# Linear attention with a running state: inter and state product in 64x32 tiles over pairs of sequences, and a new order of the steps around them

## The chip, the cores and the metric

The kernel runs on one core of a Trainium2 chip. The metric is the device time of one execution in microseconds (us), the median of the runs. A core has a matrix engine (TensorE, here PE), whose results go to PSUM banks, and VectorE (DVE), ScalarE (ACT) and GpSimd (POOL); SyncE (SP) issues DMAs. Every engine works through its own list of instructions in order and waits on semaphores.

## What is computed

Input: x of 4 sequences by 2048 tokens by 512 features. It is normalised (xn), and the result is x + attention(xn) + fp8 layer(xn):

```python
q = softmax(be * heads(xn @ Wq.T + bq));  k = softmax(be * heads(xn @ Wk.T + bk));  v = heads(xn @ Wv.T + bv)
kv = cumsum(einsum('zsD,zsd->zsDd', k, v), axis=1);  kn = cumsum(k, axis=1)      # 64 heads of 8
out = einsum('zsD,zsDd->zsd', q, kv) / sum(q * kn)
attention = out @ Wo.T + bo
ffn = fp8(clip(xn / input_scale)) @ (weight_fp8 * weight_scale).T + bias
```

## The kernel before

A step takes 32 tokens (TOK) of each of the 4 sequences (SEQS), so 128 rows; there are 64 steps. The sum over the past is split: *intra* is the product of a step's masked scores with its own values, *inter* the product of the queries with the running state (k times v and, as a ninth column, k times one, hence VW = 9, summed over all steps before). The 64 heads are held as 16 groups g of J = 4 heads: a 32x32 block transposition on DVE (`qT`, `kT`) puts 4 heads times 8 features on 32 partitions, one band of 32 partitions for each sequence.

Every engine runs `body(i)` for i = 0 to 65, each with three ages of step in flight: i (projections), t = i - 1 (scores, state, inter, intra) and i - 2 (output). PE's order in `body(i)` (L921) is: keys of i into `k_ps`, scores half 0 of t, `state(t, 0)`, transposition of the attention of i - 2 (L943), queries of i into `q_ps`, scores half 1, `state(t, 1)`, fp8 product (L975) and output product (`project_out`, L884 to L888) of i - 2 into `vo_ps`, inter of t (L999), values of i into `vo_ps` (L873 to L877 with another target), intra of t (L1018). A projection is 12 float16 matmuls of 512 columns (`project`).

- `state` (L905 to L919): for each group and sequence a 32x32 product of `k_e` and `vp` over the rows of that sequence, 36 columns; the four sequences lie on the diagonal of the array. The result holds, for each sequence's band, 4 heads against 4 heads, of which DVE keeps the diagonal (`mask_state`, L650) and adds it to `st_run` (`add_state`, L660).
- The spread (ACT, L530): `st_run` is copied four times, each time with one sequence's band kept (`seq_mask`), into `st_seqs`, so that a row of it has a block of 36 columns for each sequence.
- inter (L999): 128 rows (all sequences) by 32 columns of `qT`, with 144 columns of `st_seqs`. It writes into `a_ps`, which the state product used before it, and waits for `masked_ready`.
- intra (L1018): 64 matmuls, 128x32, of 36 columns, added to the same bank.
- The output's bias is put into `vo_ps` by ACT (L477, after the values were read), the keys' bias into `k_ps` (L489, right after the exponential of the keys).
- DVE's order in `body(i)` (L731 on): attention of i - 2 divided by its sum (L682, L690), `xn` of i + 1, quantising of i (L637), maximum and shift of k, two score masks, first state mask, `al` (low part of the attention, L748), key sums and `kT`, shift of q, `magic` (L624, L629), two score masks, `qT` (L769), second state mask, output (L720), `add_state`, statistics of i + 3, variances (each second step), values times 1/sum (`vp`, L727).
- POOL makes the low part of the input (L400), the rounding of the fp8 input (L407, L411) and the root (L385 to L391). SP issues the DMAs in a fixed order: 8 for the values of t, two transposing ones, input, output, residual.

## Time and profile before

| | |
|---|---|
| median of 3 runs | 1249.07 us (1248.55 to 1250.06) |
| profiled execution | 1248.2 us from its first to its last instruction, 60447 instructions |
| PE busy | 1174.9 us (94%) |
| DVE busy | 977.9 us (78%) |
| ACT busy | 744.9 us (60%) |
| POOL busy | 321.6 us (26%) |

The profile is one execution. Its page lists the busy time of each engine, the chain of work that ended last, and groups of instructions by line; the trace behind it can be asked for a stretch of time, an engine or a line. A matmul's record shows its latency, several hundred ns; the time that a series of them takes is read from the starts. A float32 matmul has two records, a float32 transposition one, a float16 matmul one.

### The profile page before, as it was taken

What the parts mean: (1) busy time and instruction counts of PE and PEld (TensorE: products, weight loads), DVE (VectorE), ACT (ScalarE), POOL (GpSimd) and SP (SyncE); (2) the same over time, 40 slices, a digit from 0 to 9 for tenths busy, and PEclk for the clock granted to TensorE, in tenths of its full rate; (3) what the DMA queues carried; (4) which work ended last, traced back from release to release, by engine and by line L of the source; (5) the groups of instructions that cost most, each with busy time, mean ns of one, the idle gap of its engine ahead of it and who ended that gap; (6) DMA issues with size and microseconds to landing.
All of it is one profiled execution on the core that took longest, in us unless ns stands there. A gap on an engine that the chain in (4) does not pass through costs nothing.

```text
span 1248.2 us, 60447 instructions
## 1 busy us (share of the span) xinstructions
PE 1174.9 (94%) x26082; PEld 679.2 (54%) x26082; DVE 977.9 (78%) x1968; ACT 744.9 (60%) x1177; POOL 321.6 (26%) x590
## 2 busy tenths in 40 slices
PE   1459999999999999999999999999999999999996
PEld 1235555555555555555555555555555555555553
DVE  4567887888788788878878887788788778878873
ACT  0456656665666666566666656666665666566652
POOL 3122222322222232222223232222323232222310
PEclk9689999999999999999999999999999999999999
DMA  9022334334334433433333343343343433333331
GB/s 234 21 59 70 81 90 89 78 80 91 82 82 87 89 80 79 90 86 80 85 89 82 77 90 89 78 84 91 81 79 91 84 83 81 91 82 81 72 73 46
DMA packets 156483, 104.64 MB, mean 84 GB/s; under 512 B 111968, under 2 KB 128480, under 8 KB 156256
## 3 DMA queue, kind: packets, MB, share of 16 engines
q1 hardware_dynamic: 155536, 99.76, 35.7%
q8 instruction: 209, 3.42, 1.2%
q10 hardware_dynamic: 720, 1.31, 0.4%
q14 instruction: 18, 0.15, 0.0%
HBM read 40.20 MB, written 16.78 MB: 46 GB/s over the span
## 4 chain that ended last, share of the span: by engine, by line
PE 92%; issue 3%; DVE 2%; DMA 1%; ACT 1%; POOL 1%; SPq 0%; POOLq 0%; DVEq 0%; ACTq 0%
PE s_ps L900 10%; PE a_ps L917 7%; PE a_ps L1018 6%; PE a_ps L999 6%; PE k_ps L873 5%; PE vo_ps L975 5%; PE vo_ps L873 5%; PE k_ps L877 5%; PE k_ps L875 5%; PE vo_ps L884 4%; PE vo_ps L888 4%; PE vo_ps L886 4%; PE vo_ps L877 4%; PE vo_ps L875 4%; PE q_ps L877 4%; PE q_ps L873 4%
## 5 line engine op out<-in xcount | busy, mean ns | idle before, releaser
L521 ACT ACTIVATE q_heads<-qT,cst 128x512 f32<-128x512 f32 x256 | 163.9, 711 | 88.2 <-DVE qT L769 88.2
L407 POOL TENSOR_TENSOR y_sum<-y,y_magic 128x512 f32<-128x512 f32 x64 | 81.4, 1272 | 433.0 <-DVE y_magic L629 433.0
L506 ACT ACTIVATE w_own<-kT,cst 128x512 f32<-128x512 f32 x128 | 85.5, 715 | 166.7 <-DVE kT L711 166.7
L530 ACT ACTIVATE st_seqs<-st_run,cst 128x576 f32<-128x576 f32 x252 | 181.5, 797 | 0.5 <-DVE st_run L665 0.5
L671 DVE TENSOR_TENSOR att<-s_ps,cst 128x512 f32<-128x512 f32 x256 | 163.8, 682 | 0.4 <-PE s_ps L900 0.4
L400 POOL TENSOR_TENSOR x_split<-xn,x_split 128x512 f16<-128x512 f32 x64 | 74.1, 1158 | 291.6 <-ACT x_split L462 284.3
L900 PE MATMUL s_ps<-q_heads,w_own 64*64 64x128 f32 x4096 | 141.3, 275 | 0.6 <-DVE att L671 0.6
L900 PEld LDWEIGHTS s_ps<-q_heads,w_own 64*64 64x64 f32 x4096 | 110.4, 132 | 54.3 <-issue 54.2
L462 ACT ACTIVATE x_split<-xn 128x512 f16<-128x512 f32 x64 | 40.3, 630 | 126.7 <-DVE xn L618 126.7
L873 PE MATMUL k_ps<-w_hi,xT 128*128 128x512 f16 x256 | 98.9, 386 | 17.0 <-DMA xT<-x_split 12.3
L727 DVE TENSOR_TENSOR vp<-vo_ps,vp 128x512 f32<-128x512 f32 x64 | 44.3, 692 | 86.3 <-PE vo_ps L877 86.3
L884 PE MATMUL vo_ps<-w_hi,ah 128*128 128x512 f16 x260 | 98.5, 379 | 0.6 <-DVE al L748 0.6
L888 PE MATMUL vo_ps<-w_hi,al 128*128 128x512 f16 x260 | 98.5, 379 | 0.0
L886 PE MATMUL vo_ps<-w_lo,ah 128*128 128x512 f16 x260 | 98.5, 379 | 0.0
L875 PE MATMUL k_ps<-w_lo,xT 128*128 128x512 f16 x256 | 98.3, 384 | 0.0
L877 PE MATMUL k_ps<-w_hi,xT 128*128 128x512 f16 x256 | 98.3, 384 | 0.0
L873 PE MATMUL vo_ps<-w_hi,xT 128*128 128x512 f16 x256 | 97.7, 382 | 0.0
L917 PE MATMUL a_ps<-vp,k_e 32*32 32x36 f32 x8064 | 97.6, 196 | 0.0
L873 PE MATMUL q_ps<-w_hi,xT 128*128 128x512 f16 x256 | 97.0, 379 | 0.0
L875 PE MATMUL q_ps<-w_lo,xT 128*128 128x512 f16 x256 | 97.0, 379 | 0.0
L877 PE MATMUL q_ps<-w_hi,xT 128*128 128x512 f16 x256 | 97.0, 379 | 0.0
L875 PE MATMUL vo_ps<-w_lo,xT 128*128 128x512 f16 x256 | 97.0, 379 | 0.0
(136 smaller groups left out, 2287.8 us busy)
## 6 DMA issues: line engine op xcount, KB each, us to landing
v_groups<-vp SPq DMA_DIRECT2D x512, 36.0 KB, 3.1
x_in<-L_attn_x SPq DMA_DIRECT2D x64, 256.0 KB
x_res<-L_attn_x SPq DMA_DIRECT2D x64, 256.0 KB
out<-o_sb SPq DMA_DIRECT2D x64, 256.0 KB
w_own<-L_attn_Wk SPq DMA_DIRECT2D x1, 1024.0 KB, 13.0
w_own<-L_attn_Wq SPq DMA_DIRECT2D x1, 1024.0 KB, 15.0
w_own<-L_attn_Wv SPq DMA_DIRECT2D x1, 1024.0 KB, 16.5
att<-L_ffn_weight_fp SPq DMA_DIRECT2D x1, 1024.0 KB, 18.1
```

Of the source, the lines that this page charges most:

```text
L506: last = sc.activation(k_pairs[:, i.parity, :, c, :], kT[:, :, :], ACT.Copy, scale=pair_mask[:, c:c + 1])
L521: last = sc.activation(q_heads[:, i.parity, :, j, :], qT[:, i.parity, :, :], ACT.Copy, scale=head_mask[:, j:j + 1])
L530: last = sc.activation(st_seqs[:, i.parity, :, :, b, :].rearrange("p g j w -> p (g j) w"), st_run[:, :, :, :].rearrange("p g j w -> p (g j ...
L671: v.tensor_tensor(att[:, c % 2, 4 * (c // 2):4 * (c // 2) + 4, :, :] .rearrange("p g j s -> p (g j) s"), s_ps[:, DM * (c % 2):DM * (c % 2 ...
L873: mm(bank[:, :], xT[:, t.parity, 0, c, :], w_hi[:, m, c, :], start=(c == 0 and not seeded), stop=False, skip_group_check=seeded)
L875: mm(bank[:, :], xT[:, t.parity, 0, c, :], w_lo[:, m, c, :], start=False, stop=False, skip_group_check=seeded)
L877: last = mm(bank[:, :], xT[:, t.parity, 1, c, :], w_hi[:, m, c, :], start=False, stop=(c == KC - 1), skip_group_check=seeded)
L884: mm(vo_ps[:, :], ah[:, j, :], w_hi[:, MO, j, :], start=(j == 0 and not rest), stop=False, skip_group_check=rest)
L886: mm(vo_ps[:, :], ah[:, j, :], w_lo[:, MO, j, :], start=False, stop=False, skip_group_check=rest)
L888: last = mm(vo_ps[:, :], al[:, j, :], w_hi[:, MO, j, :], start=False, stop=(j == J - 1), skip_group_check=rest)
L900: last = mm(s_ps[SP * TOK * gp:SP * TOK * (gp + 1), DM * n + P * q:DM * n + P * (q + 1)], k_pairs[rows, t.parity, g, :, :].rearrange("p c ...
L917: last = mm(a_ps[rows, col:col + J * VW], k_e[rows, t.parity, TOK * g:TOK * (g + 1)], vp[rows, t.parity, v_head(g):v_head(g) + J, :], star ...
```

## The change

- The state product is formed for pairs of sequences: 64 rows (two sequences) by 32 columns of `k_e`, with 72 columns: a new tile `v_pairs` holds the values twice, once with only the even and once with only the odd sequences' rows (`pair_mask`), so that the two come out side by side. 32 matmuls in place of 64, in one stage after scores half 0. The new rows' band is the group within its four (u), not the sequence.
- POOL makes `v_pairs` with two multiplications (`pair_values`) ahead of its other work of a step; `state` waits for them.
- `mask_state` handles both halves at once. The spread moves blocks between bands of 32 partitions: 16 small copies in place of 4 large ones, in two halves, one at the end of a body and one in the next body, after `ah`.
- inter is 32 matmuls of 64x32 with 72 columns; bank n of `a_ps` now holds a pair of sequences. intra keeps its matmuls and is called in two halves with waits of their own.
- The fp8 and the output product go into `k_ps`; the output's seed follows the exponential of the keys, and the keys' seed waits for DVE's output. `vo_ps` holds only values, which wait for `vp` of the step before.
- DVE's order: statistics ahead of `xn`; both state masks after the first score masks; variances and `magic` ahead of `al`; output ahead of `qT`; quantising for i + 1 near the end.

The diff, cut to its core:

```diff
-        st_seqs = sb("st_seqs", [P, 2, G, J, SEQS, VW])
...
+        v_pairs = w_own[0][:, :, :].rearrange("p c d -> p (c d)")[:, 0:SP * HEADS * VW]\
+            .rearrange("p (c h w) -> p c h w", c=SP, h=HEADS)
+        st_masked = sb("st_masked", [P, SEQS // SP, G // J, SP, J, VW])
+        st_run = sb("st_run", [P, SEQS // SP, G // J, SP, J, VW])
+        st_pairs = sb("st_pairs", [P, 2, G, J, SP, VW])
...
-        a_view = a_halves[:, :, 0:G // 2 * GW]
-        a_rows = a_view.rearrange("p n (l r) -> p n l r", l=GP)
+        a_view = a_halves[:, :, 0:G * SP * VW]
+        a_rows = a_view.rearrange("p n (h l j r) -> p n h l j r", h=2, l=GP, j=J)
...
+            def pair_values(t):
+                pool.wait_ge(vp_ready, (t + 1).n)
+                if t.after(1):
+                    pool.wait_ge(state_done, t.n)
+                for c in range(SP):
+                    last = gp.tensor_tensor(v_pairs[:, c].rearrange("p h w -> p (h w)"),
+                                            vp[:, t.parity].rearrange("p h w -> p (h w)"),
+                                            pair_mask[:, c:c + 1].to_broadcast([P, HEADS * VW]), ALU.mult)
+                last.then_inc(vpairs_ready, 1)
             def body(i):
...
                     low_input(i + 1)
...
@@ -465,28 +482,41 @@
...
+            def spread_state(t, seqs):
...
+                if seqs[0] == 0:
+                    act.wait_ge(strun_ready, (t + 1).n)
+                    if t.after(1):
+                        act.wait_ge(a_done, t.n)
+                    else:
+                        act.wait_ge(st_cleared, 1)
+                for b in seqs:
+                    for u in range(J):
+                        last = sc.activation(st_pairs[TOK * b:TOK * (b + 1), to, u::J, :, b % SP, :],
+                                             st_run[TOK * u:TOK * (u + 1), b // SP, :, b % SP, :, :],
+                                             ACT.Copy)
+                if seqs[-1] == SEQS - 1:
+                    last.then_inc(stpairs_ready, 1)
...
             def body(i, last_weights=None, fold=False):
-                t = i - 2
-                if t.exists():
-                    if (t + 1).exists():
-                        act.wait_ge(vp_ready, (t + 2).n)
-                    else:
-                        act.wait_ge(o_ready, t.n)
-                    if t.off == 0 and isinstance(t.k, int):
-                        act.wait_ge(fold_ready, 1)
-                    sc.activation(vo_ps[:, :], bias[:, 3, :], ACT.Copy, scale=out_up[:, :])\
-                        .then_inc(oseed_ready, 1)
+                d = i - 2
                 if (i + 1).exists():
                     high_input(i + 1)
                 if i.exists():
                     act.wait_ge(kshift_ready, (i + 1).n)
                     if i.after(2):
-                        act.wait_ge(state_done, (i - 1).n * 2)
+                        act.wait_ge(state_done, (i - 1).n)
                         act.wait_ge(kT_ready, (i - 1).n)
                     sc.activation(k_e[:, i.parity, :], k_shift[:, :], ACT.Exp, scale=k_exp_scale[:, :])\
                         .then_inc(ke_ready, 1)
-                    if (i + 1).exists():
-                        sc.activation(k_ps[:, :], bias[:, MK, :], ACT.Copy).then_inc(kseed_ready, 1)
+                if d.exists():
+                    if not i.exists():
+                        act.wait_ge(o_ready, d.n)
+                    if d.off == 0 and isinstance(d.k, int):
+                        act.wait_ge(fold_ready, 1)
+                    sc.activation(k_ps[:, :], bias[:, 3, :], ACT.Copy, scale=out_up[:, :])\
+                        .then_inc(oseed_ready, 1)
...
+                if d.exists() and (i - 1).exists():
+                    spread_state(d, range(SP, SEQS))
...
                     if (i + 1).exists():
                         sc.activation(q_ps[:, :], bias[:, MQ, :], ACT.Copy).then_inc(qseed_ready, 1)
+                        if d.exists():
+                            act.wait_ge(o_ready, (d + 1).n)
+                        sc.activation(k_ps[:, :], bias[:, MK, :], ACT.Copy).then_inc(kseed_ready, 1)
...
                     last.then_inc(qheads_ready, 1)
...
-                    for b in range(SEQS):
-                        last = sc.activation(st_seqs[:, i.parity, :, :, b, :].rearrange("p g j w -> p (g j) w"),
-                                             st_run[:, :, :, :].rearrange("p g j w -> p (g j) w"),
-                                             ACT.Copy, scale=seq_mask[:, b:b + 1])
-                    last.then_inc(stseqs_ready, 1)
+                if (i - 1).exists() and i.exists():
+                    spread_state(i - 1, range(SP))
...
-            def mask_state(t, n):
-
...
+            def mask_state(t):
+                dve.wait_ge(state_done, (t + 1).n)
+                for n in range(SEQS // SP):
+                    last = v.tensor_tensor(
+                        st_masked[:, n].rearrange("p q c j w -> p (q c) j w"),
+                        a_state[:, n, :].rearrange("p (g j w) -> p g j w", j=J, w=VW),
+                        head_mask[:, None, :, None].to_broadcast([P, G // 2, J, VW]), ALU.mult)
...
             def body(i, last_weights=None, fold=False):
-                t = i - 1
-                if (i - 2).exists():
-                    normalise_attention(i - 2)
+                t, d = i - 1, i - 2
+                if d.exists():
+                    normalise_attention(d)
+                if (i + 3).exists():
+                    statistics(i + 3)
                 if (i + 1).exists():
                     normalise(i + 1)
                 if i.exists():
-                    if i.after(1):
-                        quantise(i)
                     shift(i, k_ps, k_done, k_max, kmax_ready, k_shift, kshift_ready, ke_ready)
                 if t.exists():
                     mask_scores(t, 0)
                     mask_scores(t, 1)
-                    if i.exists():
-                        mask_state(t, 0)
-                if (i - 2).exists():
-                    dve.wait_ge(ah_ready, (i - 1).n)
-                    v.tensor_tensor(flat(al[:, :, :]), t_ps[:, :], flat(ah[:, :, :]), ALU.subtract)\
-                        .then_inc(al_ready, 1)
+                if t.exists() and i.exists():
+                    mask_state(t)
+                if i.parity == 0 and (i + PAIR).exists():
+                    variances(i + PAIR)
+                if (i + 1).exists():
+                    magic(i + 1)
+                if d.exists():
+                    split_low(d)
...
                 if i.exists():
                     key_sums(i)
+                if i.exists():
                     shift(i, q_ps, q_done, q_max, qmax_ready, q_shift, qshift_ready, qe_ready)
-                if (i + 1).exists():
-                    magic(i + 1)
                 if t.exists():
                     mask_scores(t, 2)
                     mask_scores(t, 3)
-                if i.exists():
-                    dve.wait_ge(qe_ready, (i + 1).n)
-                    if i.after(2):
-                        dve.wait_ge(qheads_ready, (i - 1).n)
-                        dve.wait_ge(a_done, (i - 1).n)
-                    v.transpose(qT[:, i.parity].rearrange("p g s -> p (g s)"), q_e[:, :]).then_inc(qT_ready, 1)
-                if t.exists() and i.exists():
-                    mask_state(t, 1)
...
-                if (i - 2).exists():
-                    output(i - 2)
+                if d.exists():
+                    output(d)
+                if i.exists():
+                    turn_queries(i)
                 if t.exists() and i.exists():
                     add_state(t)
-                if (i + 3).exists():
-                    statistics(i + 3)
-                if i.parity == 0 and (i + PAIR).exists():
-                    variances(i + PAIR)
+                if (i + 1).exists():
+                    quantise(i + 1)
                 if i.exists():
                     scale_values(i)
...
-            def state(t, n):
-
...
+            def state(t):
...
+                pe.wait_ge(ke_ready, (t + 1).n)
+                pe.wait_ge(vpairs_ready, (t + 1).n)
...
+                pe.sem_inc(pe_waited, 1)
+                for c4 in range(G // J):
+                    for u in range(J):
+                        g = J * c4 + u
+                        for n in range(SEQS // SP):
+                            rows = slice(SP * TOK * n, SP * TOK * (n + 1))
+                            col = DM * n + SP * J * VW * c4
+                            last = mm(a_ps[TOK * u:TOK * (u + 1), col:col + SP * J * VW],
+                                      k_e[rows, t.parity, TOK * g:TOK * (g + 1)],
+                                      v_pairs[rows, :, v_head(g):v_head(g) + J, :]
+                                      .rearrange("p c j w -> p c (j w)"), start=True, stop=True)
+                last.then_inc(state_done, 1)
...
+            def values(i, fold):
...
+                if i.after(1):
+                    pe.wait_ge(vp_ready, i.n)
+                project(vo_ps, i, MV, seeded=False).then_inc(v_done, 1)
...
+            def quantised(t, low_part):
...
+                pe.wait_ge(xq_turned, (t + 1).n * 16)
+                pe.wait_ge(oseed_ready, (t + 1).n)
+                for c in range(KC):
+                    last = mm(k_ps[:, :], xq[:, t.slot, c, :], w_hi[:, MF, c, :], start=False,
+                              stop=False, skip_group_check=True)
...
+            def output_product(t):
...
+                pe.wait_ge(ah_ready, (t + 1).n)
+                pe.wait_ge(al_ready, (t + 1).n)
+                project_out(k_ps, rest=True).then_inc(o_done, 1)
...
+            def inter(t, more):
+                pe.wait_ge(qT_ready, (t + 1).n)
+                if more:
+                    pe.wait_ge(masked_ready, (t + 1).n)
...
+                if t.after(1):
+                    pe.wait_ge(stpairs_ready, t.n)
+                pe.sem_inc(pe_waited, 1)
+                for h in range(2):
+                    for gp in range(GP):
+                        for u in range(J):
+                            g = G // 2 * h + GP * u + gp
+                            for n in range(SEQS // SP):
+                                rows = slice(SP * TOK * n, SP * TOK * (n + 1))
+                                mm(a_rows[TOK * u:TOK * (u + 1), n, h, gp].rearrange("p j r -> p (j r)"),
+                                   qT[rows, t.parity, g, :],
+                                   st_pairs[rows, t.parity, g].rearrange("p j c w -> p (j c w)"),
+                                   start=(h == 0 and gp == 0), stop=False, skip_group_check=True)
+            def intra(t, h):
+                pe.wait_ge(att_ready, t.n * 4 + 2 * h + 2)
+                if h == 0:
+                    for b in range(SEQS):
+                        pe.wait_ge(v_moved[t.parity][b], (t + 2).half * 16 * GP)
                     pe.sem_inc(pe_waited, 1)
...
+                for n in range(SEQS // SP):
+                    for j in range(J):
+                        for u in range(J):
+                            last = mm(a_rows[TOK * u:TOK * (u + 1), n, h, :, j, :],
+                                      att[:, n, J * h + u, j, :],
+                                      v_groups[:, t.parity, :, n, J * h + u, j, :], start=False, stop=True,
+                                      skip_group_check=True)
+                if h == 1:
+                    last.then_inc(a_done, 1)
```

## Rows read from the trace of the kernel before

**Rows 1.** Page: busy time, chain by engine; span and mean granted clock.

```profile
PE 1174.9 (94%) x26082; PEld 679.2 (54%) x26082; DVE 977.9 (78%) x1968; ACT 744.9 (60%) x1177; POOL 321.6 (26%) x590
...
PE 92%; issue 3%; DVE 2%; DMA 1%; ACT 1%; POOL 1%; SPq 0%; POOLq 0%; DVEq 0%; ACTq 0%
...
core 0: 1248.2 us, clock 0.982
```

**Rows 2.** Stretch: busy PE, PEld, DVE, ACT, POOL; PEclk, DMA share, GB/s.

```profile
500.00:600.00 100.00, 99.36 (x2261) 57.55 (x2260) 82.39 (x168) 60.95 (x97) 26.71 (x52) 1.00 0.39 88
```

**Rows 3.** PE in order of time: intra of bodies 1, 2, 63.

```profile
98.32 1.31 PE L1018 MATMUL a_ps<-v_groups,att 128*32 128x36 f32 x128
...
117.17 1.32 PE L1018 MATMUL a_ps<-v_groups,att 128*32 128x36 f32 x128
...
1223.53 1.31 PE L1018 MATMUL a_ps<-v_groups,att 128*32 128x36 f32 x128
```

**Rows 4.** As rows 2: inter, values, intra; keys to second state.

```profile
603.24:604.36 1.12, 1.12 (x33) 0.90 (x33) 1.05 (x2) 1.12 (x3) 0.51 (x1) 1.00 0.01 4
604.36:607.06 2.70, 2.70 (x17) 1.10 (x13) 1.15 (x3) 2.70 (x5) 0.00 (x0) 1.00 0.19 18
607.06:608.34 1.28, 1.28 (x129) 1.23 (x129) 0.69 (x1) 1.28 (x3) 0.00 (x0) 1.00 0.23 51
...
608.34:611.02 2.68, 2.68 (x15) 1.07 (x13) 2.12 (x6) 1.07 (x3) 0.00 (x0) 1.00 0.37 113
611.02:612.05 1.03, 1.03 (x33) 0.86 (x32) 0.89 (x2) 0.57 (x1) 0.92 (x1) 1.00 0.37 130
612.05:612.75 0.70, 0.70 (x69) 0.65 (x65) 0.70 (x2) 0.04 (x1) 0.25 (x1) 1.00 0.45 134
612.75:613.24 0.49, 0.49 (x11) 0.48 (x6) 0.49 (x2) 0.49 (x1) 0.00 (x0) 1.00 0.32 102
613.24:615.92 2.68, 2.68 (x14) 1.08 (x12) 2.15 (x4) 1.20 (x3) 0.00 (x0) 1.00 0.54 110
615.92:616.96 1.04, 1.04 (x34) 0.87 (x33) 0.91 (x2) 0.00 (x0) 0.00 (x0) 1.00 0.79 136
616.96:617.73 0.77, 0.77 (x69) 0.72 (x65) 0.77 (x2) 0.52 (x1) 0.00 (x0) 1.00 0.76 156
```

**Rows 5.** Waits from 500 to 1100 us (us in total, times, longest).

```profile
PEld s_ps L900 <- issue: 28.0, 66, 0.4
PEld a_ps L999 <- DVE qT L769: 17.8, 31, 0.7
```

**Rows 6.** Order of time around inter; DVE's first and last of a step.

```profile
602.72 0.42 DVE L654 TENSOR_TENSOR st_masked<-a_ps,cst 128x288 f32<-128x288 f32 x1
...
608.42 0.57 DVE L682 RECIPROCAL den_rec<-a_ps 128x32 f32<-128x32 f32 x2 [0.50 <-PE a_ps L1018]
...
621.01 0.42 DVE L654 TENSOR_TENSOR st_masked<-a_ps,cst 128x288 f32<-128x288 f32 x1
...
625.45 0.69 DVE L727 TENSOR_TENSOR vp<-vo_ps,vp 128x512 f32<-128x512 f32 x1 [1.09 <-PE vo_ps L877]
...
620.98 0.38 PE L888 MATMUL vo_ps<-w_hi,al 128*128 128x512 f16 x1
621.53 1.19 PE L999 MATMUL a_ps<-st_seqs,qT 128*32 128x144 f32 x32 [0.17 <-issue]
```

**Rows 7.** ACT in order of time: one column, 512 columns, the spread of a step.

```profile
4.95 0.20 ACT L454 ACTIVATE exp_beta<-scal 128x1 f32<-128x1 f32 x1 [2.94 <-DMA scal<-L_ffn_weight_scale]
...
51.70 0.58 ACT L569 ACTIVATE q_ps<-bias 128x512 f32<-128x512 f32 x1
...
605.30 2.88 ACT L530 ACTIVATE st_seqs<-st_run,cst 128x576 f32<-128x576 f32 x4
```

**Rows 8.** Groups by line on POOL (busy us, mean ns, idle before).

```profile
L407 POOL TENSOR_TENSOR y_sum<-y,y_magic 128x512 f32<-128x512 f32 x9 | 11.5, 1273 | 62.7 <-DVE y_magic L629 62.7
...
L436 POOL TENSOR_TENSOR bias<-bias,w_scale_up 128x512 f32<-128x512 f32 x2 | 2.0, 1028 | 6.9 <-issue 6.9
```

More of the change, by code:

```diff
@@ L892, in scores @@
             def scores(t, half):
+                if half == 0:
+                    pe.wait_ge(kpairs_ready, (t + 1).n)
+                    pe.wait_ge(qheads_ready, (t + 1).n)
+                    if t.after(1):
+                        pe.wait_ge(att_ready, t.n * 4)
+                else:
+                    pe.wait_ge(att_ready, t.n * 4 + 2)
                 pe.sem_inc(pe_waited, 1)
@@ new lines, in turn_attention @@
+            def turn_attention(t):
+                pe.wait_ge(an_ready, (t + 1).n)
+                if t.after(1):
+                    pe.wait_ge(al_ready, t.n)
+                else:
+                    pe.wait_ge(bvl_ready, 1)
+                for b in range(SEQS):
+                    last = transpose(t_ps[:, :].rearrange("p (j b s) -> p b j s", b=SEQS, s=TOK)[:, b],
+                                     a_n[:, b, :, :].rearrange("p g d -> p (g d)"), ident)
+                last.then_inc(aT_done, 1)
@@ L932, in body @@
                     scores(t, 0)
                     if i.exists():
[L934 to L945 removed]
+                        state(t)
@@ L946, in body @@
+                if d.exists():
+                    turn_attention(d)
                 if fold:
@@ L1024, in transpose_weights @@
+                    inter(t, i.exists())
+                if i.exists():
+                    values(i, fold)
+                if t.exists():
+                    intra(t, 0)
+                    intra(t, 1)
             def transpose_weights(m):
```

188 lines of the change are left out of this document (63 added, 125 removed).

## The prediction

> **What bounds the kernel now.** I read the page first: one engine, the matrix engine (PE), is busy 94% of the span, at a mean granted clock of 0.982, so at the higher of its two levels (2.4 GHz), and the chain that ended last is 92% PE [rows 1]. Then the busy time of a steady stretch: in 100 us PE is busy 99.36, VectorE (DVE) 82.39, ScalarE (ACT) 60.95, GpSimd (POOL) 26.71 [rows 2]. So in the loop only PE's own work counts, and everything else matters as far as it makes PE wait. The step: intra starts at 98.32 in body 1 and 1223.53 in body 63 [rows 3], that is 1125.2 us in 62 steps, 18.15 each, and without the slow first one (117.17 to 1223.53, 61 steps) 18.14. 63 bodies have all stages; the start-up ends at about 80 us.
>
> Next the stages of one step in PE's order [rows 4]: keys 2.68, scores 1.03, state 0.70, turning of the attention 0.49, queries 2.68, scores 1.04, state 0.77, then fp8 and output products (617.73 to 621.29, with the usual 0.31 from the last matmul [rows 6]: 3.56), inter 1.12, values 2.70, intra 1.28. The float16 products are untouched, at 12 matmuls of 512 columns in 2.68. The float32 stages consist of passes (two records for each float32 matmul, one for each transposition), and here the rows give a price per column: scores 32 passes of 128 columns in 1.03 us = 0.25 ns a column; inter 32 of 144 in 1.12 = 0.24; state 64 of 36 in 0.70 to 0.77 = 0.30 to 0.33; intra 128 of 36 in 1.28 = 0.28. All four spread over four tiles of the array (64x64; 128x32; the four diagonal 32x32; 128x32). The transposes take the whole array as one tile: 4 passes of 128 columns in 0.49 = 0.96 ns a column, 3.9 times the four-tile price. For the shortest passes the floor is per pass: 10.0 ns (intra), 10.9 and 12.0 ns (state).
>
> PE's only true wait in the loop is before inter: PE's load of weights is idle 17.8 us over 31 times there, 0.57 each, while at scores the idle time is 28.0 over 66, 0.42 each [rows 5]. The 0.15 beyond the usual pause are a wait. The row names the transposition of the queries (L769), but that had ended; what ends last is the second masking of the state (L654, ends 603.14, and inter starts at 603.24; in the next step ends 621.43, inter 621.53) [rows 6]. In the second of these it costs 0.24 us: the last output matmul starts at 620.98, and a change of stage elsewhere costs 0.31. I take 0.14 a step.
>
> **The change on PE.** State before: 64 matmuls = 128 passes of 36 columns in two stages, 0.70 + 0.77 = 1.47. After: 32 matmuls = 64 passes of 72 columns, in one stage. Inter before: 16 matmuls = 32 passes of 144, 1.12. After: 32 matmuls = 64 passes of 72. Both then have the same form: 4608 pass-columns in 64x32 tiles, of which the array holds eight. No row shows this form. The nearest rows bound it. If eight tiles stand to four as four to one, a column costs 0.12 and the stage 0.56; the floor per pass, 64 x 10.0 to 12.0 ns, gives 0.64 to 0.77. If the array gives no more than the four-tile price, 4608 x 0.243 = 1.12. I take 0.70, the length of the state stage that also has 64 passes [rows 4], because from one tile to four the price fell almost in proportion. So state saves 1.47 - 0.70 = 0.77, inter 1.12 - 0.70 = 0.42.
>
> The Trainium skill says the first too: "TensorEngine Tiling (Array Packing)", Tiling Modes, lists 64x32 as eight tiles that load and multiply independently; the trace bears that out up to four. Against the change speaks "TensorE: Matmul & The Clock Gate", Part 1, on the 56 ns gap, which puts matmuls never closer than about 25 ns from start to start: 64 passes would take 1.6 us, the two stages 3.2 against 2.6 now, some 0.6 us a step slower. This trace disagrees, with 128 passes in 1.28 us, so the rule gets no chance of its own.
>
> The wait of 0.14 goes, since both maskings now follow the first masks of the scores: state is done at 4.4 us of the step (below), masked by 6.2, and inter starts at 12.2. Intra keeps its 64 matmuls of the same shape. Sum for a step: 0.77 + 0.42 + 0.14 = 1.33; 18.14 becomes 16.8.
>
> **Does the rest keep up?** I lay out a new step, keys at 0: scores 2.7, state 3.7, turn 4.4, queries 4.9, scores 7.6, fp8 8.6, output 9.5, inter 12.2, values 12.9, intra 15.6, end 16.8.
>
> DVE has the same operations of the same sizes: 82.39% of 18.14 = 14.9 us, against 16.8. In its new order, with the durations of its timeline (28 rows for one step, the first and the last in [rows 6]): normalising the attention from 0.1 to 1.35, statistics to 2.4, xn to 2.8 (keys are done at 2.8), k's shift to 4.2, masks to 5.4, both state maskings to 6.2, variances (each second step, 0.6) to 6.9, magic to 7.7, al to 8.4, key sums and kT to 10.4, q's shift to 11.7, masks to 12.9, output to 13.6, qT to 14.2, state sum to 14.8, quantising to 15.3. Then it waits for the values (15.7) and for intra. The tight places for PE: al at 8.4 against the output product at 9.5, and an idle rest of 1 us in even steps. Nothing on DVE delays PE, so the reordering itself costs and gains nothing beyond the 0.14.
>
> ACT: four spreads of 576 columns, 2.88 us [rows 7], become 16 copies of 32 partitions and 144 columns. Bounds of one: 0.20 (the 1-column row) and 0.58 (512 columns) [rows 7]; linear between them 0.31. Sixteen cost 5.0 at most where the old cost 2.9: ACT goes from 11.1 to 13.2 of 16.8. The second half (after ah, at 6.4) ends by 8.9, before kT at 10.4 and before inter at 12.2; the first half follows q_heads and ends early in the next step, before xn at 2.8. Cost nothing, hidden by 3 us.
>
> K's bank: the output's seed goes in after k_e, about 5.8, against 8.6. The seed for the next keys waits for the output (13.6) and is in by 14.2, against 16.8; q_heads behind it on ACT wait for qT at 14.2 anyway and end at 16.8, against scores 2.7 later. Values no longer wait for the output, which would have been late: output done 12.3 plus 0.75 after an inter of 0.70. So this move costs nothing and keeps 0.2 from coming back.
>
> POOL: two new multiplications of 576 columns. The nearest rows are 1.03 (512, with a broadcast factor) and 1.27 (two tensors) [rows 8], so 1.16 to 1.43 each, 2.3 to 2.9 together. They start after vp, 0.4 before keys, and end by 1.9 to 2.5; state needs them at 3.7. Behind them on POOL wait the low input (its own input comes at 3.9) and so the transposing DMA, which has until 16.8. The cover is 1.2 us or more.
>
> The granted clock is 1.00 in all these stages and PE stays busy, so I expect it unchanged. Start-up: the same; in body 1 the wait before inter (0.75) goes.
>
> **Sum.** State 63 x 0.77 = 48.5, inter 64 x 0.42 = 26.9, waits 62 x 0.14 + 0.75 = 9.4: 84.8 us. The profiled span 1248.2 becomes 1163.4; the median of the runs (1249.07) is 0.9 above that span: 1164.
>
> **Rivals.**
> (a) Four-tile price. The array has four float32 streams at a time, whatever the tiles; nothing in the trace shows more than four. For it: every float32 stage fits one price per column; against it: the one-tile row. Then state saves 1.47 - 1.12 = 0.35, inter nothing: 22.1 + 9.4 = 31.5, that is 1218.
> (b) DVE becomes the bound. POOL's 2.3 us fall on DVE's busiest stretch. If DVE lost all of it, its 14.9 and 0.3 of handshakes become 17.5, and the step with them: 0.64 x 63 = 40, that is 1209. The Trainium skill's "GPSIMD Engine Reference", Key points, says that the two share their SBUF interfaces; the trace has POOL idle during most of this stretch and can't show it.
> (c) Slower: the two row bands of a column band write the same PSUM partitions, in two banks, and take turns. Each of the two stages then runs at half the four-tile price, 2.24: 4.48 against 2.59 + 0.14, or 1.75 a step, 110 us: 1359. It decides from 21 ns a pass on. Scores, with two row bands on the same partitions in two banks, cost 0.25 a column, which speaks against it.
> (d) The change doesn't do what it says: a new wait (state for POOL's pairs: their cover of 4.1 us plus 1.33 is used up at 2.7 us an operation) eats all of the gain. No change, about 1249.
>
> **Chances.** Forecast 0.57, (a) 0.27, (b) 0.10, (c) 0.03, (d) 0.03. Low end: both stages at 0.60, 12 us less, 1152. High end takes in (a) with some us for small waits: 1223. A measurement of this kernel can tell about 0.2% from no change. Faster 0.94, same 0.02, slower 0.04.
>
> **What would show it.** Stage windows of state and inter near 0.70 each (right), 1.1 (a), 2.2 (c). Intra to intra 16.8. PE still over 99% busy in the loop, DVE near 89%. If DVE is near 98% and PE has gaps before the output product or the keys, (b). If PE is idle before state behind POOL's new line, (d). Copies of 144 columns above 0.5 us, or POOL's above 2 us, would make my covers wrong.

## The result and the profile after

The changed kernel takes 1187.03 us (median of 4 runs, 1185.41 to 1187.85), the kernel before 1249.57 in the same session. The ratio is 0.9492, with a 95% interval of 0.9477 to 0.9507: 62.5 us faster, where 84.8 were forecast (1164). The forecast case was the right one, and the size is three quarters of it. The profiled span is 1185.7 us.

The page of the kernel after (busy time of PE and the others, the chain by engine, span and granted clock) answers to [rows 1]:

```profile
PE 1115.6 (94%) x24098; PEld 627.9 (53%) x24098; DVE 967.9 (82%) x1968; ACT 899.3 (76%) x1933; POOL 463.6 (39%) x717
...
PE 91%; issue 4%; DVE 2%; DMA 2%; POOL 1%; SPq 0%; ACT 0%; POOLq 0%; DVEq 0%
...
core 0: 1185.7 us, clock 0.982
```

The steady stretch, columns as in [rows 2]:

```profile
500.00:600.00 100.00, 100.00 (x2205) 55.94 (x2188) 85.42 (x177) 81.62 (x178) 42.19 (x66) 1.00 0.47 88
```

PE has no gap left in this stretch, so it still bounds the kernel. DVE is at 85%, ACT went from 61 to 82%, POOL from 27 to 42%. Intra in bodies 1 and 63, for [rows 3]:

```profile
98.64 1.31 PE L1045 MATMUL a_ps<-v_groups,att 128*32 128x36 f32 x128
...
1160.73 1.31 PE L1045 MATMUL a_ps<-v_groups,att 128*32 128x36 f32 x128
```

That is 1062.1 us in 62 steps, 17.13 each, against 18.15: the gain of a step is 1.02 where 1.33 were forecast, and 1.02 x 62 = 63 is the whole gain. The start-up and the end got longer by 0.3 us each. The stages of one step, in the order scores, state, turning, queries, then inter, values, intra (for [rows 4]):

```profile
601.14:602.18 1.04, 1.04 (x34) 0.87 (x33) 1.00 (x3) 0.63 (x2) 0.00 (x0) 1.00 0.42 133
602.18:602.99 0.81, 0.81 (x68) 0.71 (x64) 0.81 (x2) 0.81 (x3) 0.65 (x1) 1.00 0.39 132
602.99:603.48 0.49, 0.49 (x10) 0.48 (x5) 0.49 (x2) 0.49 (x2) 0.49 (x1) 1.00 0.46 139
603.48:606.17 2.69, 2.69 (x15) 1.08 (x12) 2.66 (x7) 2.62 (x8) 0.58 (x2) 1.00 0.63 142
...
610.76:611.58 0.82, 0.82 (x65) 0.71 (x65) 0.71 (x2) 0.00 (x0) 0.00 (x0) 1.00 0.19 70
611.58:614.27 2.69, 2.69 (x18) 1.08 (x12) 1.64 (x4) 2.60 (x5) 0.00 (x0) 1.00 0.18 18
614.27:615.53 1.26, 1.26 (x130) 1.21 (x129) 0.69 (x1) 1.24 (x4) 0.29 (x1) 1.00 0.16 36
```

State and inter take 0.81 and 0.82 each; all other stages are what they were. The clock is 1.00 in all of them. The waits from 500 to 1100 us (us in total, times, longest), for [rows 5]:

```profile
DVE vp L754 <- PE vo_ps L911: 35.4, 35, 1.2
ACT k_ps L550 <- DVE o_sb L747: 33.3, 35, 1.3
...
PEld s_ps L941 <- issue: 29.7, 70, 0.4
...
PEld a_ps L1030 <- issue: 14.8, 35, 0.4
```

Before inter (L1030) the load of weights now pauses 14.8 over 35 times, 0.42 each, as long as before scores (29.7 over 70). The wait before inter is gone. DVE's idle time ahead of `vp` (1.0 us a step) comes back in the experiment with the statistics and variances late. The new work of ACT and POOL, grouped by line over the same stretch (busy us, mean ns, idle before):

```profile
L496 ACT ACTIVATE st_pairs<-st_run 32x144 f32<-32x144 f32 x561 | 184.2, 328 | 6.6
...
L422 POOL TENSOR_TENSOR w_own<-vp,cst 128x576 f32<-128x576 f32 x70 | 78.8, 1147 | 177.0 <-DVE vp L754 177.0
```

### The profile page after: what moved, and what is told of

Read it like the earlier page. It is cut to its first block, busy times and chain, and to the rows that moved or that the text cites. A ratio compares the mean times of both kernels' runs of the same rounds, so it can differ in the third digit from the quotient of the medians.

```text
span 1185.7 us, 57406 instructions
## 1 busy us (share of the span) xinstructions
PE 1115.6 (94%) x24098; PEld 627.9 (53%) x24098; DVE 967.9 (82%) x1968; ACT 899.3 (76%) x1933; POOL 463.6 (39%) x717
## 4 chain that ended last, share of the span: by engine, by line
PE 91%; issue 4%; DVE 2%; DMA 2%; POOL 1%; SPq 0%; ACT 0%; POOLq 0%; DVEq 0%
PE s_ps L941 11%; PE a_ps L1045 7%; PE vo_ps L907 5%; PE k_ps L1001 5%; PE k_ps L907 5%; PE k_ps L918 5%; PE k_ps L922 5%; PE k_ps L920 5%; PE vo_ps L911 5%; PE vo_ps L909 5%; PE q_ps L909 5%; PE q_ps L911 5%; PE k_ps L911 5%; PE k_ps L909 5%; PE q_ps L907 5%; PE a_ps L1030 4%
## 5 line engine op out<-in xcount | busy, mean ns | idle before, releaser
L496 ACT ACTIVATE st_pairs<-st_run 32x144 f32<-32x144 f32 x1008 | 331.0, 328 | 11.9
L422 POOL TENSOR_TENSOR w_own<-vp,cst 128x576 f32<-128x576 f32 x126 | 141.9, 1147 | 314.0 <-DVE vp L754 314.0
L907 PE MATMUL k_ps<-w_hi,xT 128*128 128x512 f16 x256 | 99.0, 387 | 17.1 <-DMA xT<-x_split 12.3
L907 PE MATMUL vo_ps<-w_hi,xT 128*128 128x512 f16 x256 | 97.7, 382 | 1.2 <-DVE bias L808 1.2
L918 PE MATMUL k_ps<-w_hi,ah 128*128 128x512 f16 x256 | 97.0, 379 | 0.6 <-DVE al L761 0.6
L911 PE MATMUL vo_ps<-w_hi,xT 128*128 128x512 f16 x256 | 97.0, 379 | 0.0
L922 PE MATMUL k_ps<-w_hi,al 128*128 128x512 f16 x256 | 97.0, 379 | 0.0
```

What stands on the lines that cost most here:

```text
L422: last = gp.tensor_tensor(v_pairs[:, c].rearrange("p h w -> p (h w)"), vp[:, t.parity].rearrange("p h w -> p (h w)"), pair_mask[:, c:c + 1 ...
L496: last = sc.activation(st_pairs[TOK * b:TOK * (b + 1), to, u::J, :, b % SP, :], st_run[TOK * u:TOK * (u + 1), b // SP, :, b % SP, :, :], A ...
L907: mm(bank[:, :], xT[:, t.parity, 0, c, :], w_hi[:, m, c, :], start=(c == 0 and not seeded), stop=False, skip_group_check=seeded)
L911: last = mm(bank[:, :], xT[:, t.parity, 1, c, :], w_hi[:, m, c, :], start=False, stop=(c == KC - 1), skip_group_check=seeded)
L918: mm(bank[:, :], ah[:, j, :], w_hi[:, MO, j, :], start=(j == 0 and not rest), stop=False, skip_group_check=rest)
L922: last = mm(bank[:, :], al[:, j, :], w_hi[:, MO, j, :], start=False, stop=(j == J - 1), skip_group_check=rest)
```

## The experiments

All kernels are the changed one with one thing different, and what hangs on it. Each ran beside the kernel before, so I compare ratios: a ratio less 0.9492, times 1249.6, is what the edit costs against the changed kernel; over 63 steps, its price in a step. The interval of such a ratio is about 0.0015 to either side; a price is the difference of two, so it is good to about 3 us.

### The state product back in 32x32 tiles

```
for g in range(G):
    for b in range(SEQS):
        rows = slice(TOK * b, TOK * (b + 1))
        mm(a_ps[rows, col:col + J * VW], k_e[rows, ..g..], vp[rows, ..g.., :])   # 32x32, 36 columns
```

> The state product alone goes back to 32x32 tiles on the diagonal (128 passes of 36 columns, four tiles in rotation, in one stage behind the first score half; no pair multiplications on POOL; the spread of the state as two scaled copies of 576 elements). Inter keeps 64x32. Theory (the gain comes from the number of passes times the number of tiles that share the array): the state stage goes from 0.81 us back to 1.25 to 1.47, so the step from 17.08 to 17.5 to 17.75 and the time from 1187 to 1215 to 1228. Rival (most of the gain is the removed stage boundary and the wait before inter, not the tiles): the one-piece stage takes 1.0 or less and the time stays below 1200.

Measured: 1254.7 us, ratio 1.0019 (1.0004 to 1.0034), 66 us above the changed kernel. Both theories missed. The window of the stage (PE, PEld, DVE, ACT, POOL, clock):

```profile
611.65:613.04 1.39, 1.39 (x132) 1.30 (x129) 1.39 (x3) 1.39 (x4) 1.16 (x1) 1.00 0.47 144
```

1.39 for the 128 passes, within the first theory's range, but this is a short one. Of the 63 state stages of the trace 49 have no long break; they take 1.36 to 1.62, 1.47 on average, against 0.82: 0.65 a step, 41 us. The other 25 us are not in every step. In windows of 100 us:

```profile
100.00:200.00 100.00, 93.60 (x2309) 54.02 (x2309) 77.92 (x162) 52.61 (x84) 25.86 (x52) 1.00 0.36 78
...
500.00:600.00 100.00, 100.00 (x2552) 58.21 (x2551) 83.84 (x173) 56.49 (x90) 29.13 (x54) 1.00 0.41 89
...
900.00:1000.00 100.00, 96.15 (x2284) 54.63 (x2271) 79.82 (x164) 53.38 (x86) 28.08 (x54) 0.98 0.38 83
```

From 300 to 800 us PE is never idle; before and after that it has gaps. In order of time, one of them:

```profile
877.19 1.22 PE L950 MATMUL a_ps<-vp,k_e 32*32 32x36 f32 x104
...
880.53 0.40 PE L950 MATMUL a_ps<-vp,k_e 32*32 32x36 f32 x24 [2.12 <-issue]
```

The stage stops after 104 of its 128 passes for 2.12 us, in the middle of a loop that has no semaphore. So it isn't a wait on another engine. The DMA view of 876.4 to 879.9 has one packet of the queue that brings instructions (packets, MB, share):

```profile
q8 instruction: 1, 0.02, 1.7%
```

In all twelve gaps of over 0.9 us inside this kernel's state stage, such a packet of 16 KB had started 2.2 to 3.0 us before the gap ended, and itself took 0.9 to 1.5; the packets come 5 to 6 us apart on average, so chance doesn't explain it. It fits PE waiting for its next instructions where small passes use them up fastest. It is argued from times, not shown by a run that changes it, and a packet alone doesn't make a gap: the kernel before has 209 of them and no gap of 0.2 us or more inside a stage, the changed kernel 193 and three. Behind four of the breaks the granted clock stood at 0.50 for 3.4 us (from 881.5, 956.6, 1178.5 and 1219.4), and the queries took 3.7 to 4.4 there where they take 2.68.

### Inter back in 128x32 tiles

```
mm(a_rows[TOK * u:TOK * (u + 1), h, gp, :], qT[:, t.parity, g, :],
   st_pairs[:, t.parity, g] ...)          # 128 rows, 144 columns, 32 passes
```

> Inter alone goes back to 128x32 tiles (32 passes of 144 columns, four tiles in rotation), the state product keeps 64x32. Theory: the inter stage goes from 0.82 back to 1.12, the step from 17.08 to 17.38, the time from 1187 to about 1206. Rival (the stages of 64 passes cost as much as 32 passes of twice the columns, and inter's part of the gain came from the wait before it): no change beyond 3 us.

Measured: 1204.7 us, ratio 0.9635 (0.9618 to 0.9652), 17.9 us above: 0.28 a step. A hit for the theory. The stage:

```profile
600.14:601.26 1.12, 1.12 (x34) 0.90 (x33) 1.12 (x3) 0.48 (x2) 0.80 (x5) 1.00 0.26 102
```

### The two row bands one after the other

```
-for c4 ...: for u ...: for n in range(2): mm(...)
+for n in range(2): for c4 ...: for u ...: mm(...)     # state; the same in inter
```

> The same 64x32 matmuls in state and inter, but all of the upper pair of sequences first, then all of the lower pair: only four tiles stand next to each other in rotation instead of eight. Theory (a matmul waits for its own tile, and TensorE doesn't reach past some few instructions, so the rate is that of the tiles in rotation): both stages go from 0.82 to about 1.1, the step to 17.65, the time to 1220 to 1225. Rival (only the number of passes and columns counts, whichever tiles they use): no change, 1187.

Measured: 1207.9 us, ratio 0.9658 (0.9642 to 0.9675), 20.7 us above: 0.33 a step. The windows of inter and of state:

```profile
601.64:602.63 0.99, 0.99 (x66) 0.89 (x65) 0.99 (x3) 0.28 (x2) 0.71 (x4) 1.00 0.24 93
610.29:611.28 0.99, 0.99 (x68) 0.89 (x64) 0.99 (x2) 0.99 (x3) 0.82 (x1) 1.00 0.41 133
```

The direction is the theory's, the size is half of it: the same matmuls, with four tiles in turn and not eight, take 0.99 and not 0.81. So the order in the program counts, and TensorE doesn't make up for it; that fits eight tiles running beside each other. One rival isn't excluded: the two row bands write two PSUM banks, so this edit also makes 32 matmuls in a row write the same bank, where in the changed kernel the bank alternates from one to the next. No run here changes one without the other. But four tiles at 72 columns were already below the 1.12 that I had taken as the four-tile price.

### Half of the columns

```
-last = mm(a_ps[.., col:col + SP * J * VW], .., v_pairs[rows, :, ..])
+last = mm(a_ps[.., col:col + J * VW],      .., v_pairs[rows, 0, ..])    # 36 of 72 columns
```

> Each of the 64 state matmuls computes only the first 36 of its 72 columns; the second sequence's half of the state is left out. It sizes a pass. If a pass costs by its columns, the stage of 0.81 us goes to about 0.45 and the time to 1164; if a pass of a 64x32 tile has a floor near 8.4 ns whatever its columns, the stage goes to about 0.65 and the time to 1177; if the floor is the whole 12.8 ns, nothing changes.

Measured: 1180.0 us, ratio 0.9435 (0.9419 to 0.9450), 7.1 us below. The stage:

```profile
613.86:614.55 0.69, 0.69 (x68) 0.65 (x64) 0.57 (x2) 0.69 (x2) 0.18 (x1) 1.00 0.46 149
```

64 passes of 36 columns take 0.69 on eight tiles and 0.70 on four [rows 4]. At this width the number of tiles gives nothing, and half of the columns take only 0.12 off 0.81. So most of the 10.8 ns of a pass doesn't go by its columns. It is the middle case of the expectation, with the floor at 10.8 and not 8.4; whether still fewer columns would go below it wasn't tried.

### Inter split in two

```
inter(t, True, halves=range(1))        # 32 passes
six of the values' twelve matmuls
inter(t, True, halves=range(1, 2))     # 32 passes
the other six
```

> The 64 inter passes are split: 32, then six of the values' twelve matmuls, then the other 32, then the other six. It asks whether a short burst of small tiles goes faster than a long one. If the first some 30 passes of a stage are quick (prepared while a long matmul ran) and the rest slow, the two parts take 0.35 to 0.40 each and the step gets shorter by up to 0.1, the time is 1181 to 1187. Rival (a pass costs 12.8 ns wherever it stands, and each entry into small tiles some 0.1): the step gets longer by 0.1, the time is 1190 to 1195.

Measured: 1222.8 us, ratio 0.9787 (0.9764 to 0.9811), 36.9 us above. The first three of the four parts (inter, values, inter):

```profile
606.69:607.10 0.41, 0.41 (x33) 0.30 (x33) 0.30 (x1) 0.00 (x0) 0.00 (x0) 1.00 0.17 65
607.10:608.50 1.40, 1.40 (x15) 0.51 (x6) 1.40 (x3) 0.90 (x2) 0.00 (x0) 1.00 0.00 0
608.50:608.92 0.42, 0.42 (x34) 0.31 (x33) 0.42 (x2) 0.42 (x2) 0.00 (x0) 1.00 0.05 15
```

0.41 and 0.42: the cost is linear in the passes, 12.8 to 13.1 ns each, and a short burst is no faster. The second entry costs 0.11, in the values (2 x 1.40 against 2.69). That is 7 us, as the rival had it. The other 30 are again mostly gaps in the middle of a stage, now intra (23.6 us over the trace, against the changed kernel) and the keys behind it (3.4):

```profile
152.23 1.16 PE L1048 MATMUL a_ps<-v_groups,att 128*32 128x36 f32 x110
154.67 0.36 PE L1048 MATMUL a_ps<-v_groups,att 128*32 128x36 f32 x18 [1.28 <-issue]
```

These, too, ended 2.2 to 2.7 us after an instruction packet had started, all eighteen of them; they stand between 150 and 470 us, and none comes behind that.

### Fp8 and output products back in the values' bank

```
-mm(k_ps[:, :], xq..., w_hi[:, MF ...])        +mm(vo_ps[:, :], ...)
 values():                                     +pe.wait_ge(o_ready, (i - 1).n)
```

> The fp8 and output products go back to the values' PSUM bank, all else as in the changed kernel. Theory (by the prediction, the move keeps a wait from coming back: the output's eviction must be done before the values' projection starts, and inter is now only 0.8 long): values wait 0.1 to 0.2 us in each step, 1193 to 1199. Rival (inter covers the eviction): no change, 1187.

Measured: 1225.2 us, ratio 0.9786 (0.9768 to 0.9804), 36.7 us above, far over both. Inter, the eviction of the output and the values, in order of time:

```profile
613.42 0.88 PE L1033 MATMUL a_ps<-st_pairs,qT 64*32 64x72 f32 x64
613.66 0.74 DVE L748 SCALAR_TENSOR_TENSOR o_sb<-vo_ps,out_dn,x_res 128x512 f32<-128x512 f32 x1
614.55 0.38 PE L908 MATMUL vo_ps<-w_hi,xT 128*128 128x512 f16 x1 [0.24 <-DVE o_sb L748]
```

From inter to values it is 1.13 here and 0.82 in the changed kernel. In half of the steps the eviction starts 0.11 behind inter and the distance is 1.01; in every fourth it starts some 0.7 behind and the distance is about 1.6. The mean is 1.17, so the wait costs 0.35 a step, 22 us. The intra stage is longer as well, by 15 us over the trace, by breaks like those above; why they come more often in this kernel stays open. The two make up the whole 37.

### VectorE's order: all of it, and parts

The whole old order, with only the state's masks left early:

```
normalise_attention, normalise, quantise(i), shift K, mask_scores x2, mask_state, split_low, key_sums, shift Q,
magic, mask_scores x2, turn_queries, output, add_state, statistics, variances, scale_values
```

> VectorE goes back to the order of the kernel before, with the one exception that both masks of the state stay ahead of the key shift's followers, where the changed kernel has them. Theory (the reordering itself is worth nothing, as predicted): 1187 within 3. Rival (the reordering covers waits that the shorter step would bring): each 0.1 us of wait in a step is 6 us, 1193 or more.

Measured: 1209.9 us, ratio 0.9667 (0.9651 to 0.9683), 21.9 us above. The theory of no effect, which is the prediction's, is wrong. Every second step takes 17.9 to 18.0, the others 17.1. In a long one (POOL's last root operation, its pair multiplications, `xn` on DVE, the state product on PE):

```profile
609.46 0.20 POOL L393 TENSOR_TENSOR rstd<-newton 128x2 f32<-128x2 f32 x1
609.60 2.43 POOL L422 TENSOR_TENSOR w_own<-vp,cst 128x576 f32<-128x576 f32 x2
609.69 1.34 DVE L645 TENSOR_SCALAR xn<-x_in,mv,rstd 128x512 f32<-128x512 f32 x1 [0.59 <-POOL rstd L393]
...
612.14 0.88 PE L958 MATMUL a_ps<-w_own,k_e 64*32 64x72 f32 x64 [0.71 <-issue]
```

The state product starts when POOL's pairs end (612.03), and the pairs start when the root ends. And `xn`, which itself waited 0.59 for the root, takes 1.34 beside them where it takes 0.55 in the changed kernel. So there were two suspects, and three parts to tell them apart.

Only the variances late:

```
-    variances(i + PAIR)        # behind mask_state
+    variances(i + PAIR)        # ahead of scale_values
```

> The changed kernel with one thing moved: VectorE's four small variance operations, which every second step start the eight POOL operations of the inverse root, go from behind the state's masks back to the end of the step. In the run with VectorE's whole old order every second step is 0.9 us longer, and POOL's root (606.44 to 609.66) stands there ahead of the pair multiplications (609.60 to 612.03), after which the state product starts (612.14). Theory (the reordering pays because it takes POOL's root out of the pair multiplications' way): every second step is longer by 0.7 to 0.9 again, the time is 1208 to 1214. Rival (what costs is VectorE's slower operations on memory beside POOL, 1.34 us for the normalisation where it was 0.55): no change from 1187, or under 1195.

Measured: 1192.6 us, ratio 0.9541 (0.9525 to 0.9557), 6.1 us above: between the theory and its rival. Every fourth step is 0.4 longer, the others 0.1 at most. The root is in the way here too, but ends earlier than in the whole old order (keys, root, pairs and state product of one step):

```profile
601.07 0.39 PE L907 MATMUL k_ps<-w_hi,xT 128*128 128x512 f16 x1
...
602.33 0.19 POOL L393 TENSOR_TENSOR rstd<-newton 128x2 f32<-128x2 f32 x1
...
602.48 2.25 POOL L422 TENSOR_TENSOR w_own<-vp,cst 128x576 f32<-128x576 f32 x2
...
604.83 0.88 PE L959 MATMUL a_ps<-w_own,k_e 64*32 64x72 f32 x64
```

Only the statistics behind the masks:

```
-    statistics(i + 3)          # ahead of normalise
+    statistics(i + 3)          # behind mask_state
```

> The changed kernel with only VectorE's batch statistics moved, from the start of the step to behind the state's masks, so that the normalisation runs right behind the attention's, beside POOL's pair multiplications. Theory of the contention: the normalisation takes 0.9 to 1.3 us instead of 0.55, the pair multiplications 1.2 instead of 1.15; since K's shift comes no later than before (0.86 us of statistics went from in front of it), the time stays at 1187 within 3. Rival (the statistics' place is a part of the reordering's gain): 1193 or more. If the normalisation stays at 0.55, POOL and VectorE don't slow each other, and the 1.34 has another cause.

Measured: 1185.4 us, ratio 0.9482 (0.9466 to 0.9498), no difference. DVE's row for `xn` from 500 to 1100 us:

```profile
L645 DVE TENSOR_SCALAR xn<-x_in,mv,rstd 128x512 f32<-128x512 f32 x35 | 27.5, 786 | 0.0
```

0.79 and not 0.55, and the time is the same. DVE does lose time beside POOL, but that alone costs nothing.

Statistics and variances both late:

```
     add_state(t)
+    statistics(i + 3)
+    variances(i + PAIR)
     quantise(i + 1)
     scale_values(i)
```

> The changed kernel with both the batch statistics and the four variance operations of VectorE at the end of the step, behind the state's addition; the quantisation keeps its new place. It asks what made the 22 us of VectorE's whole old order, of which the variances alone gave 5 and the statistics moved to the middle none. Theory (VectorE has 1.16 us of idle time ahead of the values' scaling; statistics of 0.86 fit in there, statistics and variances of 1.4 to 1.5 don't, so in every second step the values are scaled late, and POOL's root and pair multiplications start later still): every second step is 0.6 to 0.9 longer, the time is 1204 to 1212. Rival (it is the quantisation ahead of K's shift, on top of the variances): 1192 to 1195, as with the variances alone.

Measured: 1218.6 us, ratio 0.9740 (0.9723 to 0.9756), 31 us above, more than the range given and more than the whole old order. In a long step:

```profile
610.51 0.17 DVE L636 TENSOR_SCALAR guess<-shifted 128x2 int32<-128x2 int32 x1
...
610.76 0.33 POOL L387 TENSOR_TENSOR newton<-guess 128x2 f32<-128x2 f32 x1 [6.36 <-DVE guess L636]
610.96 0.68 DVE L754 TENSOR_TENSOR vp<-vo_ps,vp 128x512 f32<-128x512 f32 x1
...
615.16 1.33 POOL L422 TENSOR_TENSOR w_own<-vp,cst 128x576 f32<-128x576 f32 x1
...
616.58 0.87 PE L959 MATMUL a_ps<-w_own,k_e 64*32 64x72 f32 x64 [1.03 <-issue]
```

The guess comes at 610.51, so POOL's root of some 3 us stands ahead of the pairs, though `vp` ended at 611.64. The last pair operation ends just before the state product starts. The mechanism is that of the theory: the reordering pays because it takes the root out of the way of the pairs. What sizes the three losses is when the root ends, counted from the start of the step's keys: 1.5 with the variances alone late, 2.0 to 2.2 with the whole old order, mostly 2.3 to 2.4 here. From there it is 2.3 to 2.5 to the state product (the pairs and 0.1), which in the changed kernel starts 3.7 behind the keys: so it starts at 3.8 to 4.1, 4.6 to 4.7 and 4.8 to 4.9 in those steps, at 6, 22 and 31 us. In every long step of the three kernels the state product starts 0.1 behind the end of the pairs; in the changed kernel 1.8 lie between. In every second step here `vp` also ends 0.3 to 0.4 later against the keys, as the theory had it.

### The state's masks late

```
 turn_queries(i)
+mask_state(t)
 add_state(t)
```

> The changed kernel with the two masks of the state moved behind the transposition of the queries on VectorE, just ahead of the state's addition. Theory (inter may not overwrite the state product before it is masked, so it waits for both masks): inter waits 1.3 to 1.9 us in each step, the time is 1265 to 1305. Rival (there is cover of about a mask, so only part shows): below 1240.

Measured: 1398.2 us, ratio 1.1174 (1.1148 to 1.1200), 210 us above, double the expectation. The stretch without work before inter, and the one behind it:

```profile
607.50:609.85 2.35, 0.13 (x2) 0.03 (x2) 2.15 (x5) 1.38 (x3) 0.38 (x2) 1.00 0.07 21
609.85:613.45 3.60, 3.60 (x71) 1.78 (x72) 1.02 (x2) 3.54 (x9) 0.00 (x0) 0.53 0.25 44
```

The mechanism is the expected one: inter waits for the masks, 2.3 us a step and so more than the 1.9 at most of the expectation. But a third of the price is another: behind the idle 2.35 the granted clock stands at 0.53, near the lower of its two levels (1.2 GHz), and inter and five of the values' matmuls run at half speed: 1.1 us in a step on average.

### POOL's pairs twice

```
-for c in range(SP):
+for c in (0, 1, 0, 1):      # with a wait for the first two ahead of the second two
```

> POOL makes its pair multiplications twice (four of 1.15 us instead of two). The product of the first two is overwritten by the same values. Theory (two are done 1.85 us before the state product starts, four are done 0.4 to 0.5 us after that): the state product waits 0.4 to 0.5 us in each step, 1212 to 1218, and VectorE's operations that run beside them get no longer. Rival (VectorE and POOL share their access to memory, and VectorE has little slack): VectorE's busy time grows by over 0.5 us in a step and the time exceeds 1225. Second rival: no change, the cover is larger than read.

Measured: 1233.3 us, ratio 0.9860 (0.9843 to 0.9876), 46 us above: 0.73 a step. PE around the state product, and POOL's group:

```profile
602.54 1.10 PE L945 MATMUL s_ps<-q_heads,w_own 64*64 64x128 f32 x32
604.34 0.88 PE L963 MATMUL a_ps<-w_own,k_e 64*32 64x72 f32 x64 [0.70 <-issue]
...
L426 POOL TENSOR_TENSOR w_own<-vp,cst 128x576 f32<-128x576 f32 x133 | 155.7, 1191 | 187.2 <-DVE vp L758 184.7
```

The wait is there, at 0.73 and not 0.4 to 0.5, since the added work (two of 1.19 and a handshake) is 2.5 us, against a cover of 1.85 (pairs done at 600.33, state at 602.18 in the changed kernel). PE waits 0.77 a step in the trace. Of DVE's operations only `xn`, which now runs beside the second two, got longer (0.88 on average, from 0.55).

No kernel here beats the changed one; the one at 1180.0 leaves out half of the state.

## Why the prediction was right, and where its sizes were wrong

**The case.** The forecast rested on one choice: that the array runs eight 64x32 tiles beside each other, so that the new stages are shorter than at the four-tile price. Shorter they are, and rival (a), with inter at 1.12, was wrong: 0.82 in the window, and 1.12 again with the old tiles. That eight tiles are the reason rests on the run with the bands apart, where the gain shrinks by a third; the alternation of the PSUM banks goes with it and isn't told apart. Rival (c), bands taking turns on the same partitions, is excluded by the same window.

**The term that was mis-sized: 0.70 for a stage.** I took the row of state's first stage because it has 64 passes, and left aside that its passes have 36 columns. At 36 columns the changed shape takes 0.69; the other 36 cost 0.12. It measured 0.81 and 0.82, which is 0.11 and 0.12 more, 14 us in all. The range of 0.56 to 1.12 held it. Neither bound was a law: with the eight-tile price per column the stage would be 0.56, with the floor per pass 0.69, and both together give more than either.

**State before: 1.47.** The second of its stages was read from one step (0.77). Another step of the kernel before:

```profile
562.64 0.76 PE L917 MATMUL a_ps<-vp,k_e 32*32 32x36 f32 x64
563.33 1.04 PE L975 MATMUL vo_ps<-w_hi,xq 128*128 128x512 f16 x4
```

0.69 from start to start. Over all 63 steps the two stages take 0.72 and 0.70 on average, with 0.69 in most. So state was 1.42 before and saved 0.59, not 0.77: 0.05 of that is this row, the rest the stage. Run alone in one stage, the old shape takes 1.47 on average, so merging the stages as such gave nothing.

**Inter.** 1.12 - 0.82 = 0.30 against 0.42, and 0.28 from the run that undoes it.

**The wait before inter.** Taken at 0.14. It is gone, and the distance from scores to inter shrank by 0.17 on average (3.73 to 3.56). With 0.59 and 0.30 that makes 1.06; intra is 0.03 longer on average, and the step measured 1.02.

**K's bank.** Right that the move costs nothing; ACT's new seed waits 33.3 us over 35 times, 0.95 each, at no price. The value of what it prevents was 0.35 and not 0.2. In half of the steps the forecast holds (the eviction starts 0.11 behind inter's start, PE waits 0.19), but in a quarter of them it starts 0.2 behind and in a quarter 0.7; and PE starts 0.15 behind its end, which the sum left out.

**VectorE's order.** Here a step of the prediction failed, though it left no mark on the time, since the changed kernel has the new order. It followed DVE's operations against PE and found no wait, and it said that the reordering itself gains nothing. It didn't follow what DVE's operations release on POOL. There the root and the new pair multiplications share one queue, and the old order would have put them in a row ahead of the state product, at 22 us.

**Covers.** POOL 1.15 an operation, against 1.16 to 1.43; its cover 1.85, against "1.2 or more". ACT's copies 0.33, against 0.31 at most; 16 are 5.3 us, still hidden. DVE 14.6 us a step, against 14.9; ACT 14.0, against 13.2. Rival (b) had its cause but not its effect: DVE's `xn` goes from 0.55 to 0.79 beside POOL's pairs, and in the changed kernel the two don't meet, since statistics stand between. The Trainium skill's "GPSIMD Engine Reference", Key points, says that the two share their interfaces to SBUF; these rows agree.

**Clock and start-up.** As forecast.

## What to carry to other kernels

Small float32 matmuls gain from more tiles in rotation only above some width: here nothing at 36 columns, 0.18 of 0.99 us at 72, if neighbours in the program lie in different row bands (and so, here, in different PSUM banks). Price such a stage from a row with the same passes *and* the same columns, or measure one, and take its length before from several steps. When an engine is given new work in a queue that it shares with old work, follow what releases the old work: here four tiny operations on another engine, at their old place, would have cost 6 us, and 31 together with the statistics.

## What the runs showed of the hardware that I had not expected

- Time of a pass, in stages of 64 passes at full clock: 10.8 ns (36 columns, eight tiles), 10.9 (36, four), 12.8 (72, eight), 15.5 (72, four); 32 passes of 144 on four tiles, 35.0. In stages of 128 passes of 36 on four tiles: 9.8 (128x32, intra), 11.5 on average (32x32 on the diagonal). The Trainium skill, "TensorE: Matmul & The Clock Gate", Part 1, has about 25 ns from start to start as the least; the runs disagree.
- Stages of small passes can stop in the middle with no semaphore near, for 0.2 to 2.3 us. In two kernels this cost 25 to 30 us, in a third 15. The changed kernel itself has three of 0.2 us or more, the kernel before none. They end 2.2 to 3.0 us after the start of a 16 KB instruction packet. That the fetch is the cause wasn't tried.
- An idle PE of 2.35 us lowered the clock to 0.53 for the next 3.6 us, which added half again to the price of the wait.
- `xn` (512 columns, all operands in SBUF) took 0.55 alone, 0.79 where it met POOL's multiplications in part, and up to 1.34 in full; operations that read PSUM kept their length.
